# One semaphore per weight group, and an earlier first norm, in a recurrent layer with a gated MLP on eight cores

## The reference

```python
n  = layernorm(x)
xn = n * rsqrt(mean(n * n) + 1e-6) * norm_w
u  = (xn @ in_w.T + in_b) * sigmoid(xn @ gate_w.T + gate_b)
b, c, d = u @ b_w.T + b_b, u @ c_w.T + c_b, u @ d_w.T + d_b
h[t] = a * h[t-1] + b[t]
y  = (c * h + d) @ out_w.T + out_b
x1 = x + n + y
g, v = layernorm(x1) @ w_gate.T, layernorm(x1) @ w_up.T
out = x1 + (silu(g / 127) * (v / 127)) @ w_down.T / 127
```

## Time and profile before

| what | us |
|---|---|
| median of the two timed runs | 3838.48 |
| the two timed runs | 3708.34 and 3968.62 |
| the profiled execution | 3545.59 |
| its span, slowest core (core 7) | 3543.9 |
| its fastest core (core 1) | 3531.2 |
| busy in the span: PE, DVE, ACT | 3174.7, 1062.7, 536.9 |

### The profile page before, as it was taken

One profiled execution on the slowest core, in us unless ns is written; L12 is line 12 of the kernel. 1 busy time (PEld: TensorE's weight loads), 2 busy tenths in 40 slices (PEclk: granted clock), 3 DMA queues, 4 the chain that ended last, 5 costly groups with the idle time before them and its releaser, 6 DMA issues.

```text
span 3543.9 us, 40730 instructions; the slowest of 8 cores (3531.2 to 3543.9 us)
## 1 busy us (share of the span) xinstructions
PE 3174.7 (90%) x14208; PEld 1396.7 (39%) x14208; DVE 1062.7 (30%) x1546; ACT 536.9 (15%) x794; POOL 202.9 (6%) x388
## 2 busy tenths in 40 slices
PE   2887777899889989899898998899998998989989
PEld 0333322344334434344343443344443443434434
DVE  3221312322342231422323323422324223242231
ACT  1110111111111112111121111111111111211110
POOL 0011010000100001000010001000010000100010
PEclk8999998999999999999999999999999999999999
DMA  5999998553445434454345434454334542445334
GB/s 107 200 210 216 208 215 185 190 154 125 137 156 177 152 110 137 161 176 145 107 149 181 152 114 136 165 168 154 125 131 155 173 155 98 146 161 155 114 130 131
DMA packets 153846, 545.88 MB, mean 154 GB/s; under 512 B 17456, under 2 KB 17456, under 8 KB 153648
## 3 DMA queue, kind: packets, MB, share of 16 engines
q1 hardware_dynamic: 98352, 325.16, 27.7%
q0 software_dynamic: 55296, 218.13, 24.6%
HBM read 526.44 MB, written 73.40 MB: 169 GB/s over the span
## 4 chain that ended last, share of the span: by engine, by line
PE 77%; DMA 15%; DVE 6%; issue 1%; ACT 1%; DVEq 0%; SPq 0%; POOLq 0%; ACTq 0%; POOL 0%
PE pb L273 77%; DMA s_wa<-dw_wd 3%; DMA s_wa<-dw_wfu 2%; DMA cw_wfu<-s_wa 2%; DMA cw_wd<-s_wa 2%; DMA s_wa<-cw_wfd 1%; DVE s_xn L535 1%; DMA s_x<-x 1%; DVE s_sr L533 1%; DMA s_wa<-dw_wug_g 1%; DMA s_wa<-dw_wout 1%; DVE s_xn L356 1%; DMA cw_wfd<-s_wa 1%; DMA cw_wug_g<-s_wa 1%; DVE s_sr L349 1%
## 5 line engine op out<-in xcount | busy, mean ns | idle before, releaser
L273 PE MATMUL pb<-s_uy,s_wa 128*128 128x512 bf16 x8704 | 1911.0, 380 | 99.9 <-DMA s_wa<-dw_wfd 16.3
L273 PE MATMUL pb<-s_xn,s_wa 128*128 128x512 bf16 x5120 | 1184.7, 393 | 214.6 <-DVE s_xn L356 89.8
L273 PEld LDWEIGHTS pb<-s_uy,s_wa 128*128 128x128 bf16 x8704 | 848.3, 98 | 1152.7 <-issue 151.1
L273 PEld LDWEIGHTS pb<-s_xn,s_wa 128*128 128x128 bf16 x5120 | 511.1, 100 | 887.5 <-issue 327.6
L568 DVE SCALAR_TENSOR_TENSOR s_uy<-pb,s_gsb 128x512 bf16<-128x512 f32 x192 | 132.8, 692 | 582.9 <-PE pb L273 582.9
L441 DVE TENSOR_TENSOR_SCAN s_hs<-s_a,s_h,s_bsb 128x512 f32<-128x512 f32 x128 | 164.3, 1284 | 446.6 <-ACT s_bsb L436 445.4
L415 DVE SCALAR_TENSOR_TENSOR s_uy<-pb,s_bias,s_gsb 128x512 bf16<-128x512 f32 x128 | 96.1, 751 | 388.9 <-ACT s_gsb L410 388.9
L436 ACT ACTIVATE s_bsb<-pb,s_bias 128x512 f32<-128x512 f32 x128 | 88.0, 687 | 817.0 <-PE pb L273 817.0
L564 ACT ACTIVATE s_gsb<-pb 128x512 f32<-128x512 f32 x192 | 114.6, 597 | 569.5 <-PE pb L273 569.4
L471 DVE SCALAR_TENSOR_TENSOR s_uy<-pb,s_bias,s_yv 128x512 bf16<-128x512 f32 x128 | 96.1, 751 | 263.5 <-PE pb L273 263.5
L468 DVE TENSOR_TENSOR s_yv<-s_csb,s_hs 128x512 f32<-128x512 f32 x128 | 88.6, 692 | 258.1 <-ACT s_csb L451 258.1
(11 more groups left out here) (44 smaller groups left out, 643.8 us busy)
## 6 DMA issues: line engine op xcount, KB each, us to landing
s_wa<-cw_wb SPq DMA_DIRECT2D x112, 512.0 KB, 3.8
s_wa<-cw_wc SPq DMA_DIRECT2D x112, 512.0 KB, 3.8
s_wa<-cw_wd SPq DMA_DIRECT2D x112, 512.0 KB, 3.9
s_wa<-cw_wfg POOLq DMA_DIRECT2D x84, 512.0 KB, 4.2
s_wa<-cw_wfu POOLq DMA_DIRECT2D x84, 512.0 KB, 4.9
s_wa<-cw_wfd POOLq DMA_DIRECT2D x56, 768.0 KB, 5.7
s_wa<-cw_wug_in SPq DMA_DIRECT2D x56, 512.0 KB, 3.9
s_wa<-cw_wug_g SPq DMA_DIRECT2D x56, 512.0 KB, 4.6
```

The source lines that it names most:

```text
L273: lambda t: t.matmul(pbank[bi][:], lh, rh, start=st, stop=sp))(),
```

## The change

Five edits, all in the code that writes the order; what is computed stays the same.

1. **One semaphore per group of loads.** `alloc_sem` gives a semaphore, and the two loads of a group of wug or of wfg and wfu, or the three of wb, wc and wd, now share it (`sem=sp`). PE waits once per group, for the last of the loads: `tok_wug_g[gg]`, `tok_wd[j]`, `tok_wfu[gh]` at the group's first matmul.
2. **Merged bank releases.** A bank that ACT reads is now free when the DVE operation that ends the step is done, and the down loop waits for fewer of the `tok_h`.
3. **The first norm moves.** The sums stand at jh = 12 of the MLP, the squares go from ACT to DVE (`emit_sq1`, one behind each of jh = 14 to 21), the tail stands after j = 0 of the down loop, and the f blocks are done by j = 4: `fb_ops` has the difference, the product and s_xn, `fb_w` the residual s_w, and `FB_SCHED` says what stands after which step.
4. **The copy of x1** goes from DVE to ACT, in front of the square.
5. The residual is written behind s_xn rather than ahead of it.

```diff
+    def alloc_sem(self, fam):
...
+    def dma(self, stream, fn, waits=(), sem=None):
+        if sem is None:
+            sem = self.alloc_sem("G" if stream == "G" else "Q")
         prev = [(sem, self.cnt[sem])] if self.cnt[sem] else []
         return self.emit(stream, fn, waits, inc=sem, amt=16, forced=prev, is_dma=True)
...
-            for f in range(DK):
-                st["tok_sq"].append(em.emit("S", (lambda f=f: lambda s: s.activation(
-                    s_xbf[:, f], s_xbf[:, f], AF.Square))(),
-                    waits=[tok_summ[f]], inc="S"))
+        def emit_sq1(st, f):
+            st["tok_sq"][f] = em.emit("V", (lambda f=f: lambda v: v.tensor_mul(
+                s_xbf[:, f], s_xbf[:, f], s_xbf[:, f]))(),
+                waits=[st["tok_summ"][f]], inc="V")
...
+        FB_SCHED = [["f0", "f1", "w0"], ["f2", "w1", "f3", "w2"],
+                    ["f4", "w3", "f5", "w4"], ["f6", "w5", "f7", "w6", "w7"]]
...
                 if jg % 2 == 1 and gg + 2 < DK:
                     g2 = gg + 2
-                    tok_wug_i[g2] = load_w("wug_in", g2, g2, c)
-                    tok_wug_g[g2] = load_w("wug_g", g2, g2, c)
+                    sp = em.alloc_sem("G" if c == 0 else "Q")
+                    tok_wug_i[g2] = load_w("wug_in", g2, g2, c, sem=sp)
+                    tok_wug_g[g2] = load_w("wug_g", g2, g2, c, sem=sp)
...
                     mm(bb_, wview("wb", j, IK)[:, k, :], u_v[:, k, :], k == 0, k == IK - 1,
-                       waits=[tok_wb[j], tok_u[-1]] if k == 0 else [], inc=(k == IK - 1))
+                       waits=[tok_wd[j], tok_u[-1]] if k == 0 else [], inc=(k == IK - 1))
...
                 if j + 2 < IK:
                     j2 = j + 2
-                    tok_wb[j2] = load_w("wb", j2, j2, c)
-                    tok_wc[j2] = load_w("wc", j2, j2, c)
-                    tok_wd[j2] = load_w("wd", j2, j2, c)
+                    sp = em.alloc_sem("G" if c == 0 else "Q")
+                    tok_wb[j2] = load_w("wb", j2, j2, c, sem=sp)
+                    tok_wc[j2] = load_w("wc", j2, j2, c, sem=sp)
+                    tok_wd[j2] = load_w("wd", j2, j2, c, sem=sp)
...
+                banks[bb_].r = tok_y[j]
+                banks[bc_].r = tok_y[j]
                 banks[bd_].r = tok_y[j]
...
-                banks[bo].r = tok_x1[j]
-                tok_cp2[j] = em.emit("V", (lambda j=j: lambda v: v.tensor_copy(
-                    ua0[:, j], s_x1[:, j]))(), inc="V")
+                tok_cp2[j] = em.emit("S", (lambda j=j: lambda s: s.activation(
+                    ua0[:, j], s_x1[:, j], AF.Identity))(),
+                    waits=[tok_x1[j]], inc="S")
+                banks[bo].r = tok_cp2[j]
...
+                if st_next is not None and jh == 12:
+                    emit_stats1_mms(st_next)
...
+                if st_next is not None and 14 <= jh < 14 + DK:
+                    emit_sq1(st_next, jh - 14)
...
                 if st_next is not None:
-                    if j == 1:
+                    if j == 0:
                         emit_stats1_tail(st_next)
-                    elif j >= 2:
-                        emit_f_block(st_next, j - 2)
+                    elif j - 1 < len(FB_SCHED):
+                        for task in FB_SCHED[j - 1]:
+                            if task[0] == "f":
+                                fb_ops(st_next, int(task[1]))
+                            else:
+                                fb_w(st_next, int(task[1]))
 
             if st_next is not None:
-                emit_f_block(st_next, 6)
-                emit_f_block(st_next, 7)
                 st_next["wb"], st_next["wc"], st_next["wd"] = {}, {}, {}
                 for j in range(2):
-                    st_next["wb"][j] = load_w("wb", j, j, c + 1)
...
+                    sp = em.alloc_sem("Q")
+                    st_next["wb"][j] = load_w("wb", j, j, c + 1, sem=sp)
```

More of the change, by code:

```diff
@@ L26 @@
 NQ = 8
-DMA_SEMS = {f"G{i}" for i in range(NG)} | {f"Q{i}" for i in range(NQ)}
 SEM_NAMES = (["T", "V", "S", "Gc"] + [f"G{i}" for i in range(NG)]
@@ L90, in emit @@
         return tok
-    def dma(self, stream, fn, waits=()):
-        if stream == "G":
+    def alloc_sem(self, fam):
+        if fam == "G":
             sem = f"G{self.g_rr % NG}"
@@ L228, in load_w @@
                 tok = em.dma("G", (lambda dst=slot_flat(slot), role=role, unit=unit:
[L229 removed]
+                                   lambda g: g.dma_start(dst, dw[role][unit]))(),
+                             waits=ws, sem=sem)
                 pending_wb[(role, slot)] = (unit, tok)
@@ L233, in load_w @@
                                            unit=unit: lambda g: g.dma_start(dst, cw[role][unit]))(),
-                             waits=ws)
+                             waits=ws, sem=sem)
             return tok
@@ L366, in build_nc @@
         for gg in range(2):
-            st_cur["wug_i"][gg] = load_w("wug_in", gg, gg, 0)
-            st_cur["wug_g"][gg] = load_w("wug_g", gg, gg, 0)
+            sp = em.alloc_sem("G")
+            st_cur["wug_i"][gg] = load_w("wug_in", gg, gg, 0, sem=sp)
+            st_cur["wug_g"][gg] = load_w("wug_g", gg, gg, 0, sem=sp)
         emit_stats1_mms(st_cur)
+        for f in range(DK):
+            emit_sq1(st_cur, f)
         emit_stats1_tail(st_cur)
         for f in range(DK):
-            emit_f_block(st_cur, f)
+            fb_ops(st_cur, f)
+            fb_w(st_cur, f)
         st_cur["wb"], st_cur["wc"], st_cur["wd"] = {}, {}, {}
         for j in range(2):
-            st_cur["wb"][j] = load_w("wb", j, j, 0)
-            st_cur["wc"][j] = load_w("wc", j, j, 0)
-            st_cur["wd"][j] = load_w("wd", j, j, 0)
+            sp = em.alloc_sem("G")
+            st_cur["wb"][j] = load_w("wb", j, j, 0, sem=sp)
+            st_cur["wc"][j] = load_w("wc", j, j, 0, sem=sp)
+            st_cur["wd"][j] = load_w("wd", j, j, 0, sem=sp)
         wug_in = s_wa[:, 0:4096].rearrange("p (b k j) -> p b k j", b=2, k=DK)
@@ L395, in build_nc @@
                        k == 0, k == DK - 1,
-                       waits=([tok_wug_i[gg], tok_xn[k]] if jg == 0 else
-                              ([tok_wug_i[gg]] if k == 0 else [])),
+                       waits=([tok_wug_g[gg], tok_xn[k]] if jg == 0 else
+                              ([tok_wug_g[gg]] if k == 0 else [])),
                        inc=(k == DK - 1))
@@ L524, in build_nc @@
             for gh in range(2):
-                tok_wfg[gh] = load_w("wfg", gh, gh, c)
-                tok_wfu[gh] = load_w("wfu", gh, gh, c)
+                sp = em.alloc_sem("G")
+                tok_wfg[gh] = load_w("wfg", gh, gh, c, sem=sp)
+                tok_wfu[gh] = load_w("wfu", gh, gh, c, sem=sp)
             tok_wfd = {}
@@ L549, in build_nc @@
                        k == 0, k == DK - 1,
-                       waits=([tok_wfg[gh], tok_xn2[k]] if jh == 0 else
-                              ([tok_wfg[gh]] if k == 0 else [])),
+                       waits=([tok_wfu[gh], tok_xn2[k]] if jh == 0 else
+                              ([tok_wfu[gh]] if k == 0 else [])),
                        inc=(k == DK - 1))
@@ L561, in build_nc @@
                     g2 = gh + 2
-                    tok_wfg[g2] = load_w("wfg", g2, g2, c)
-                    tok_wfu[g2] = load_w("wfu", g2, g2, c)
+                    sp = em.alloc_sem("G")
+                    tok_wfg[g2] = load_w("wfg", g2, g2, c, sem=sp)
+                    tok_wfu[g2] = load_w("wfu", g2, g2, c, sem=sp)
+                if st_next is not None and jh == 12:
+                    emit_stats1_mms(st_next)
                 tok_silu = em.emit("S", (lambda jh=jh, bg_=bg_: lambda s: s.activation(
@@ L578, in build_nc @@
                 for gg in range(2):
-                    st_next["wug_i"][gg] = load_w("wug_in", gg, gg, c + 1)
-                    st_next["wug_g"][gg] = load_w("wug_g", gg, gg, c + 1)
-                emit_stats1_mms(st_next)
+                    sp = em.alloc_sem("Q")
+                    st_next["wug_i"][gg] = load_w("wug_in", gg, gg, c + 1, sem=sp)
+                    st_next["wug_g"][gg] = load_w("wug_g", gg, gg, c + 1, sem=sp)
             tok_x2 = [None] * DK
```

42 lines of the change are left out of this document (21 added, 21 removed).

## The result

| | before | after |
|---|---|---|
| median of the runs, us | 3549.51 (10 runs) | 3696.42 (11 runs) |
| lowest, us | 3545.17 | 3686.02 |
| ratio, 95% interval | | 1.042 [1.0395, 1.0444] |
| profiled execution, us (span) | 3545.6 (3543.9) | 3690.6 (3688.9) |

The change makes the kernel 4.2% slower. On the footing of the profiled execution the prediction said +90 us and the profile shows +145.

The account below looks back on a forecast made before the run. It took PE, busy 90% of the span, as the bound, and weight loads in chunk 0. Terms: 3545.6 + 78 - 51 + 12 + 49 + 2 = 3635.6; that +90 on the timed median 3838.5 gave 3928 us, range 3640 to 4090.

Parts of the forecast that it names:

- the six later boundaries: Chunk boundaries after the first, with their input phases: a 9.9 us wait each for serial loads, +5 us net in all.
- the MLP: MLP of chunks 1 to 7: wfu issued only when wfg has landed, 1.7 us a chunk, +12 us.
- the down loops: Down loops of chunks 1 to 7: f blocks delay x2, step j = 7 starts 2 us late, +12 us.
- chunk 0's input phase: Six groups of serial cast loads, one gap each, partly PE's own time: +5 us (0 to 11).
- The upper bound of 14: PE's wait for wug_g at group 2 of the input phase: 9.9 us, at most 14 if landings take 3.9.
- The clock's 2.4 us: Input phase at chunk boundaries: 2.4 us lost to the lower clock behind PE's idle time would stay.
- chunk 0's recurrence: Serial cast loads leave gaps in the queue, 3.1 us a group over 13 groups: +41 us (0 to 47).
- The start: Before chunk 0's input matmuls: x lands near 29 us, PE runs on at 71 instead of 82.4: -11 us.
- The hidden chain: Rival at chunk boundaries: serial loads land before PE needs group 2, so the kernel gets faster, 3469 us; chance 0.14.
- the filled gaps: Rival in chunk 0: write-backs fill the gaps between cast loads, total within 2%, 3574 us; chance 0.23.
- The much slower case: Rival: MLP loads take 5.0 us each and all chunk 0 gaps stay open, 3713 us; chance 0.15.
- The clock's rival: Rival in chunk 0: longer PE waits drop the clock to 1.2 GHz, +42 us over 13 groups, 3678; chance 0.05.

Follow-up runs that it names:

- run 7: Changed kernel, semaphores still shared, but PE waits for each load where it first reads it (fine wait): 3647.45 us, ratio 1.028.
- run 8: Changed kernel with a semaphore per load, PE still waiting for all of a group's loads at its first matmul (coarse wait): lowest 3548.74 us, no ratio.
- Run 3: Kernel before with the moved norm and the squares on DVE alone, every load with its own semaphore: 3513.49 us, ratio 0.990.
- run 10: Kernel before, with shared semaphores and the wait for the last load for the first ten cast loads only: 3530.81 us, ratio 0.9949.
- runs 11 and 12: Changed kernel, own semaphores except first ten casts, f blocks over seven down steps: ratio 0.987; the second also moves recurrence loads behind group 2's: lowest 3483.64 us.

## Why the prediction was right and wrong

The sign, the mechanism and the place of the largest wait were right: SP's issues came 3 to 7 us apart, PE waited for wug_g 14 us into each input phase, the wait for s_xn L356 went but for chunk 0, and a wait for x2 came ahead of the last down step.

The step that failed is the base: *"The timed runs lie higher, median 3838.5, 293 above it. The change is in waits of fixed length, so I carry the difference over as it is: 3928."* That median is of two runs. Ten runs give 3549.51 for the kernel before, so the base was 289 us too high; the profiled execution's own time (3545.59) would have been the right one. The range reached the measured time only because its lower end stood on it.

Under that error lies a second one: the terms came to +90 and measured +145. Four of them carry the 55 us: the six later boundaries (18.6 short), the MLP (13.8), the down loops (13.7) and chunk 0's input phase (12.9).

*"that is 3.4 + 3.2 + 4.5 + 3.2 + 4.5 + 3.2 = 22.0"*, and a wait of 9.9 us. (With six hops of 0.1 and the 1.2 this is 23.8, not 23.9.) At the end of chunk 2 the six steps measured 4.05, 3.29, 6.95, 3.42, 4.79 and 3.4: 25.9, and 27.4 with the head of 1.5. The wait was 13.63. On average over chunks 2 to 7 the wait was 13.0, which is 3.1 more than forecast and accounts for the 3.0 by which each later boundary lost more than forecast (3.9 against 0.9). The largest mis-sized step is the pair wd and wb: 6.95 here and 5.8 on average over the six boundaries, instead of 4.5. Here wb landed 6.15 us after its issue. The first packet of the pair moved 1.9 us after the issue of wd, where it is 0.9 us for the pair of wd and wug_in. The rest of the 3.1 is spread over the other steps, each 0.2 to 0.6 us longer on average than forecast. The upper bound of 14 held, and at the first boundary the wait was 19.05 where 19 was forecast. The Trainium skill (DMA: Bandwidth & Descriptors, the anatomy of one DMA) gives a DMA a fixed 2.0 us beside its transfer, which is an estimated 3.2 for 512 KB. That fit is for DMAs that GpSimd issues, and these are SP's; their steps of 3.29, 3.42 and 3.4 come near it all the same, and the averages of 3.4 to 4.0 show that it is a floor.

*"The clock's 2.4 us stay: a pause of about the same length has only moved"*. Nearly so. Before, the 64 matmuls of groups 0 and 1 took 25.7 - 9.0 = 16.7 us; now they take 13.98. Of the stretch from group 2 to the recurrence, 43.4 us before, chunks 2 to 7 now have 46.1 on average, of which 0.4 is other new waits. So 2.7 us were gained ahead of the pause, and 2.2 lost behind it by the clock (granted 0.50 over the first 3.4 us behind the 13.63, the lower of its two levels).

*"I take 1.7 a chunk"* for the MLP; it was 3.7. Before, the 32 matmuls of a group start 6.91 us after those of the last; now such starts are late by 21.3 us in all over seven chunks, 3.1 in chunk 2. The sum asked for the right event, the end of the pair, but its pieces were off both ways, and the lateness isn't the same for each group. In chunk 2 the loads landed faster than 4.2, in 3.4 to 3.6 us for wfg and 3.5 to 4.4 for wfu, but for one of 4.9 and one of 5.2. POOL, on the other hand, took 0.53 and 0.59 us from a release to the issue behind it. For the pair that PE waits for at 1467.58 that makes 5.2 + 0.53 + 3.50 + 0.59 + 4.22 + 0.25 = 14.3 against 13.8, and the trace has 0.45 of waiting there; the pair with the 5.2 cost 1.30.

What the runs add is that neither half does it alone. Serial loads with fine waits (run 7) have an MLP of 96 to 97 us in four of chunks 1 to 6 and of 98.6 in two, parallel loads with the coarse wait (run 8) 96.1 to 97.1 in all six. Only the two together have 99.4 to 103.8 (slowest core of each).

*"j = 7 starts 2 us late"*. It was 3.0 on average (2.76 of waiting for x2 in chunk 2), and in two of the chunks the last step then took 6.9 and 8.0 us instead of 5.2, at the lower clock. Run 3, with the norm alone, shows the same wait (2.81), so this is the norm's and not the loads'. Chunk 7, which has no next norm, lost 3.4 us in this loop as well: its waits for wfd came to 3.5 us instead of 0.8.

*"Input phase: six groups, one gap each, part of it PE's own time: +5"*. It was +17.9, of which PE's wait for dw_wug_g grew by 17.5 us (12.1 to 29.6). No such part was hidden: two loads in series take longer than PE's group, as in the recurrence phase, where I had counted every gap.

*"I take 3.1 a group, 13 groups, +41"* for chunk 0's recurrence; it was +48.5. In the 12 groups that the loads paced before too it was 2.6 a group, or 31 us. The other 17 are groups 1 to 3, which before ran at PE's own 10.4 us and now take 13.8, 16.3 and 18.3: with the loads in series they pace PE from the second group on, and the prediction left these groups out. The period is near the forecast of 17 us, by another way (the chain that ended last: start, us, what):

```profile
213.73 8.31 DMA s_wa<-dw_wb
...
222.69 6.35 DMA s_wa<-dw_wc
...
230.31 8.52 DMA s_wa<-dw_wb
...
239.47 6.21 DMA s_wa<-dw_wc
```

From one wb to the next it is 16.6 us, two landings of 8.4 and 6.3 with 1.9 of issue. wd is not in the chain: the next group's wb goes out 0.6 us behind it, and wd lands in 6.5 us, before that wb does. So two loads, not three, stand in series per group.

*The start* was better than forecast: the last x tile landed at 26.4 us, not near 29, and PE runs on at 64.7, not at 71.

```profile
64.74 10.57 PE L278 MATMUL pb<-s_xn,s_wa 128*128 128x512 bf16 x40 [2.66 <-DVE s_xn L358]
```

The 5 us for eight squares in a row on DVE, which I had set against the gain, were too many: run 10, without them, runs on 2.8 us earlier. It also shows that the gain is the ten loads' alone.

*The rivals.* The hidden chain (3469) fell by the 13.63, and the filled gaps (3574) by the DMA share of 0.79. The much slower case (3713) came nearer to the profiled 3690.6 than the forecast's own 3635.6, with half of it right: its open gaps, 76 us for the input phase, recurrence and MLP of chunk 0, measured 78.8, but its +73 for the later MLPs were 25.8. The clock's rival was half true:

```profile
219.85 13.24 PE L278 MATMUL pb<-s_uy,s_wa 128*128 128x512 bf16 x48 [6.16 <-DMA s_wa<-dw_wd]
236.47 13.46 PE L278 MATMUL pb<-s_uy,s_wa 128*128 128x512 bf16 x48 [3.39 <-DMA s_wa<-dw_wd]
```

Behind each wait 48 matmuls take 13.2 to 13.5 us instead of 10.4. But the period stays at 13.24 + 3.39 = 16.6, the loads' own, and no matmul stands in the chain above: the lower clock fills time in which PE would have waited. The Trainium skill (TensorE: Matmul & The Clock Gate, HAM oscillation) describes this loop; the rows agree, and show that it is free as long as the loads set the pace.

Two things stay open. One is whether runs 11 and 12 beat the norm alone by the 29 us between their lowest runs (3484) and its median (3513): their intervals don't settle it, and 15 to 18 us of it would be what the first ten loads are worth in run 10. The other is why the packets of the pair wd and wb start 1.9 us after the issue, and those of the pair wd and wug_in after 0.9.
